# Attention with an int8 product behind it: two key tiles in one burst, and another order of scores and maxima

## The chip, the cores and the metric

The kernel runs on one core of one Trainium2 chip. The metric is the device time of one execution in microseconds, as the median of the runs. TensorE (PE in the profile, its weight loads PEld), VectorE (DVE), ScalarE (ACT), GpSimd (POOL) and SyncE (SP) each work through their own queue in order and wait for each other by semaphores.

## The reference

Eight batches of x, each 512 x 1024 (channels x positions), are projected with three weight matrices over the channels; attention with 16 heads of 32 channels and a mask over the keys follows; its result, seen as 512 rows of 1024, goes through a product with 1024 x 1024 int8 weights, each row quantised to int8 first, and x is added.

```python
Q, K, V = proj(Wq), proj(Wk), proj(Wv)          # "oc,bct->bto", then B,H,T,Dh
att = einsum("bhqd,bhkd->bhqk", Q, K) / sqrt(Dh) + b[0]
att = softmax(att * m + (1 - m) * -1e30, axis=-1)
y = einsum("bhqk,bhkd->bhqd", att, V)           # back to B, C, T
scale = max(abs(y).max(-1), 1e-7) / 127         # one row: one channel, 1024 positions
q = clip(round(y / scale), -128, 127)
out = x + float16((q @ weight.T) * scale * w_scale + bias)
```

## The kernel before

A first part (`project`) makes Q, K and V of all batches; it isn't touched. The second part (`attend`) has 32 steps, each one batch and a group of four heads. In a step there are 64 score units: two halves of 512 queries, eight key tiles of 128 keys, four heads. A unit is one matmul into one of three score banks (`scores`, L689), whose contraction runs over 100 rows: three parts of q and k, the mask's bias and two rows with the row maxima, so that the exponential (`exps`, ScalarE, L798) can be taken straight from the bank. A unit may use a bank again when the exponential three units before is done. A key tile of four exponentials is then multiplied with V by eight narrow matmuls of 32 columns that share the array (`weigh`, L716, a "burst"): a burst for tile k stands behind the last unit of tile k+1.

The row maxima for the step after are found beside that. For each of 32 pairs (head and 128 queries) two matmuls over 512 keys each (`row_max`, L127) fill one of two buffers of 1024 columns, called the ring, and VectorE reduces it to one column (`reduce_max`, L136). 64 maxima matmuls, or slots, thus stand beside the 64 units: unit, slot, unit, slot, with the bursts between. The ring's buffers are used in turn, and four more uses a step ("extras") take a turn too: the row sums of the halves (`sum_rows`, L726 and L729, behind slots SUMS_1 = 23 for the step before and SUMS_0 = 55), the turn of the int8 rows (`turn_q`, L740, behind 47) and the last product (`ffn`, L749, behind 51). A use waits until the use two before it has been read.

Half of the maxima (16 columns of 128 queries) are complete behind slots 19 and 51. With the row sums TensorE turns them (`turn_max`, L734); ScalarE takes a high part (`high_max`, L803), VectorE the rest (`low_max`, L878), and SP stores both as rows of `q_stack` (`store_max`, L609: two transfers of 16 runs of 512 B). Units 0 and 32 wait for the landing. ScalarE's queue also holds the copies of the weighted sums (`take_y`, L808), the rounding of the rows (`round_rows`, L814, behind units 37 and 39), their conversion (`make_ints`, L820, behind 41 and 43) and the issues of the loads for the next steps, of q behind units 24 to 26 and 38 to 40. VectorE's queue holds the reciprocals of the sums (`recip`, L885 and L888), their spreading (`spread`, L894, four slots behind the sums), the absolute maxima (L899) and the products' scaling (L922). GpSimd sums the exponentials of key tiles (L988), begins transfers that add a tile to another (L972, each waits for a burst) and normalises (L1007) and finishes the rows (L1013, L1016).

All orders are written out by hand: each engine has a function `step` that goes through t = 0 to 63.

Of the kernel before, what the change touches and what calls it, by code (L numbers as in the profile page):

```python
# [25 lines left out]
P = 128  # L26
# [36 lines left out]
SUMS_1, TURN_Q, FFN, SUMS_0 = 23, 47, 51, 55  # L63
# [3 lines left out]
SCORES = 3  # L67

# [7 lines left out]
def score_bank(t):  # L76

    return (t - (t > SUMS_1)) % SCORES


def score_before(t):

    if t == SUMS_1 + 1:
        return t - 1
    return t - 4 if SUMS_1 + 1 < t < SUMS_1 + 1 + SCORES else t - SCORES

# [417 lines left out]
def attend(nc, x, qk_d, v_d, bias_d, fw, ws_rep, fb_rep, out,  # L504
# [3 lines left out]
    with ExitStack() as ctx:  # L508
# [38 lines left out]
        maxT_done = sem("maxT_done")  # L547
# [8 lines left out]
        max_lo_done = sem("max_lo_done")  # L556
        recip_done = sem("recip_done")
# [15 lines left out]
        MAX_ROWS = 16 * 2  # L573
# [30 lines left out]
        def _(sp):  # L604
            def store_max(par, chunk):

                for part, rows in ((0, max_hi), (1, max_lo)):
                    dst = q_stack[par][ROW_MAX + part:ROW_MAX + part + 1, chunk, :, :]
                    sp.dma_start(dst.bitcast(F32), rows[:, chunk, :].bitcast(F32)).then_inc(max_rows[chunk], 16)  # L609
# [3 lines left out]
            def step(s, par, prev=True, main=True, ahead=True):  # L613
                if main:
                    sp.wait_ge(max_hi_done, 2 * s + 2)
                    sp.wait_ge(max_lo_done, 2 * s + 2)
                    store_max(par, 1)
                if ahead:
                    sp.wait_ge(max_hi_done, 2 * s + 3)
                    sp.wait_ge(max_lo_done, 2 * s + 3)  # L620
                    store_max(1 - par, 0)
# [21 lines left out]
        def _(pe):  # L643
            def taken(s, use):

                kind, t = use
                if not isinstance(s, int):
                    return True
                if kind == "max":
                    return 0 <= max_of_slot(s, t)[0] < STEPS  # L650
                return s < STEPS if t == SUMS_0 else 0 <= s <= STEPS if t == SUMS_1 else 0 <= s - 1 < STEPS

            def wait_ring(s, use):
# [5 lines left out]
                elif t in (SUMS_1, SUMS_0):  # L659
                    wait(pe, sums_out, 2 * s + (t == SUMS_0))  # L660
                    if not isinstance(s, int) or s + (t == SUMS_0) < STEPS:
                        pe.wait_ge(max_lo_done, 2 * s + (2 if t == SUMS_1 else 3))
# [5 lines left out]
            def take_ring(s, par, use):  # L668

                if isinstance(s, int) and (s < 0 or s == 0 and PLACE[use] < 2):  # L670
                    pe.wait_ge(neg_max_done, EARLY)
                    wait(pe, max_lo_done, s + 1)
# [78 lines left out]

            def step(s, par, prev=True, main=True, ahead=True):
                for t in range(UNITS):
                    if main:
                        scores(s, par, t)
                    if has_max(t, main, ahead):
                        next_max(s, par, t)
                    if t == GH - 1 and prev:
                        weigh(s - 1, 1 - par, QH * TT - 1)
                    if t % GH == GH - 1 and t > GH and main:  # L760
                        weigh(s, par, t // GH - 1)
                    use = ("extra", t)
                    if t == SUMS_1 and (prev or main):
                        buf = take_ring(s, par, use)
                        if main:
                            turn_max(s, 1, buf)
                        if prev:
                            sum_rows(s - 1, 1, buf)
                    if t == SUMS_0 and (main or ahead):
                        buf = take_ring(s, par, use)  # L770
                        if ahead:
                            turn_max(s + 1, 0, buf)
                        if main:
                            sum_rows(s, 0, buf)
                    if t == TURN_Q and prev:
                        turn_q(s - 1, take_ring(s, par, use))
                    if t == FFN and prev:
                        ffn(s - 1, take_ring(s, par, use))

            pe.wait_ge(const_set, 5)  # L780
# [3 lines left out]
        def _(act):  # L784
# [60 lines left out]
            def step(s, par, prev=True, main=True, ahead=True):  # L845
                for t in range(UNITS):
# [15 lines left out]
                    if t == SUMS_0 and ahead:  # L862
                        high_max(s + 1, 0, ring_of(par, ("extra", SUMS_0)))

            act.wait_ge(const_set, 5)
# [5 lines left out]
        def _(dve):  # L871
# [4 lines left out]
            def low_max(s, chunk, buf):  # L876
# [220 lines left out]
```

## Time and profile before

| | |
|---|---|
| median of 3 runs | 2441.62 us (2440.1 to 2443.0) |
| the profiled execution | 2440.84 us, of which the span is 2439.0 us |
| TensorE busy | 2387.2 us, 98% of the span |
| GpSimd, VectorE, ScalarE busy | 1672.1 us (69%), 1560.4 us (64%), 1346.3 us (55%) |
| granted clock of TensorE, mean | 0.993 |

The span is one execution as the profiler saw it, from its first to its last instruction. Busy time of TensorE is made of modelled ends of matmuls that overlap, so that distances between starts say more than lengths do. The steps of `attend` begin at 571.46 us.

### The profile page before, as it was taken

To read this page: it belongs to the slowest core of one execution; us is meant where nothing else is said; L and a number is where in the kernel's file an instruction comes from. 1 tells how busy PE (TensorE), PEld (TensorE's weight loads), DVE (VectorE), ACT (ScalarE), POOL (GpSimd) and SP (SyncE) were. 2 spreads that over 40 slices of the span, in tenths; PEclk is the share of its full clock that TensorE was granted. 3 is DMA by queue.
4 is the path that set the end of the run, shared out by engine and by line. 5 is a ranking of instruction groups with operands and counts; after the bars stand their busy time and mean duration, and the time that the engine had idled before them with its cause. 6 is when DMAs were issued, how large, how long until landed. Compare 5 with 4: busy or idle time off the path is not lost.

```text
span 2439.0 us, 37390 instructions
## 1 busy us (share of the span) xinstructions
PE 2387.2 (98%) x12376; PEld 1341.0 (55%) x12376; DVE 1560.4 (64%) x1683; ACT 1346.3 (55%) x2536; POOL 1672.1 (69%) x677
## 2 busy tenths in 40 slices
PE   8999999997999999999999999999999999999996
PEld 7888888884444444444444444444444444444442
DVE  3311111145777777777777777777777877777771
ACT  3222222214666666666666666666666666666664
POOL 3322223414778888888877888888788888887777
PEclk9999999998999999999999999999999999999999
DMA  6655555365677776777677777666776667776751
GB/s 243 252 200 199 214 193 195 147 211 126 147 160 160 157 157 147 157 159 159 151 159 159 156 160 156 157 151 150 160 160 155 155 150 160 160 155 154 157 111 44
DMA packets 143498, 396.55 MB, mean 163 GB/s; under 512 B 14584, under 2 KB 50424, under 8 KB 127296
## 3 DMA queue, kind: packets, MB, share of 16 engines
q0 software_dynamic: 18144, 132.13, 27.4%
q10 hardware_dynamic: 49312, 130.80, 22.8%
q1 hardware_dynamic: 75968, 132.74, 14.9%
q8 instruction: 34, 0.56, 0.1%
q14 instruction: 40, 0.33, 0.0%
HBM read 161.51 MB, written 100.93 MB: 108 GB/s over the span
## 4 chain that ended last, share of the span: by engine, by line
PE 67%; DMA 4%; issue 2%; POOL 2%; DVE 2%; ACT 0%; SPq 0%; ACTq 0%; POOLq 0%; DVEq 0%
PE score L689 21%; PE pv L716 18%; PE ring L127 18%; PE ring L749 4%; DMA q_stack<-max_lo 4%; PE ring L726 2%; PE ring L729 2%; DVE neg_max L136 1%; PE ring L740 1%; POOL acc L988 1%; PE ring L734 0%; DMA probs<-probs 0%; POOL acc L1000 0%; ACT probs L798 0%; SPq L609 0%
## 5 line engine op out<-in xcount | busy, mean ns | idle before, releaser
L798 ACT ACTIVATE probs<-score 128x512 f32<-128x512 f32 x2048 | 1074.7, 604 | 576.4 <-PE score L689 559.5
L136 DVE TENSOR_REDUCE neg_max<-ring 128x1 f32<-128x1024 f32 x1024 | 1208.4, 1220 | 230.8 <-PE ring L127 219.1
L689 PE MATMUL score<-q_stack,k_stack 100*128 100x512 f32 x2048 | 875.8, 429 | 23.9 <-DMA q_stack<-max_lo 16.6
L988 POOL TENSOR_TENSOR acc<-acc,probs 128x2048 f32<-128x2048 f32 x189 | 867.1, 4588 | 26.6 <-DMA probs<-probs 11.9
L127 PE MATMUL ring<-k_stack,q_stack 98*128 98x512 f32 x2048 | 810.6, 396 | 0.3 <-DVE neg_max L136 0.2
L689 PEld LDWEIGHTS score<-q_stack,k_stack 100*128 100x128 f32 x2048 | 387.3, 189 | 504.0 <-ACT probs L798 358.2
L716 PE MATMUL pv<-probs,v_in 128*32 128x512 f32 x4096 | 546.1, 605 | 0.0
L127 PEld LDWEIGHTS ring<-k_stack,q_stack 98*128 98x128 f32 x2048 | 390.8, 191 | 66.6 <-DVE neg_max L136 0.8
L988 POOL TENSOR_TENSOR acc<-probs 128x2048 f32<-128x2048 f32 x63 | 288.8, 4584 | 100.8 <-DMA probs<-probs 100.8
L479 POOL TENSOR_TENSOR q_stack<-x_raw,k_stack 128x1024 fp32r<-128x1024 f32 x28 | 67.7, 2450 | 294.7 <-ACT k_stack L364 294.7
L972 POOL DMA_DIRECT2D probs<-probs x126 | 108.2, 859 | 175.4 <-PE pv L716 168.2
L716 PEld LDWEIGHTS pv<-probs,v_in 128*32 128x32 f32 x4096 | 80.6, 108 | 184.7 <-ACT probs L798 162.6
L435 DVE TENSOR_TENSOR part_lo<-score,part_hi 128x512 fp32r<-128x512 f32 x24 | 16.4, 691 | 178.7 <-ACT part_hi L389 178.7
L491 POOL TENSOR_TENSOR part_lo<-k_scaled,part_hi 128x512 fp32r<-128x512 f32 x64 | 82.1, 1301 | 56.2 <-ACT part_hi L392 56.2
L749 PE MATMUL ring<-fw,qT 128*128 128x512 bf16 x512 | 117.8, 384 | 0.9 <-DVE qT L917 0.9
L1013 POOL TENSOR_TENSOR half<-prod,fb_rep 128x512 f16<-128x512 f32 x64 | 81.4, 1272 | 47.9 <-DVE prod L922 47.9
L291 PE MATMUL ring<-k_stack,w_hi 128*128 128x512 f32 x256 | 101.1, 395 | 0.0
L291 PE MATMUL ring<-k_stack,w_lo 128*128 128x512 f32 x256 | 101.1, 395 | 0.0
L291 PE MATMUL ring<-q_stack,w_hi 128*128 128x512 f32 x256 | 101.1, 395 | 0.0
L392 ACT ACTIVATE part_hi<-k_scaled 128x512 fp32r<-128x512 f32 x64 | 38.9, 628 | 111.3 <-DVE k_scaled L446 76.4
L885 DVE STREAM_TRANSPOSE sums_turned<-ring 128x512 f32<-128x512 f32 x64 | 45.9, 717 | 84.6 <-PE ring L729 84.6
L922 DVE SCALAR_TENSOR_TENSOR prod<-ring,scale,ws_rep 128x512 f32<-128x512 f32 x64 | 48.1, 751 | 80.8 <-PE ring L749 80.8
(95 smaller groups left out, 2026.6 us busy)
## 6 DMA issues: line engine op xcount, KB each, us to landing
probs<-probs POOLq DMA_DIRECT2D x126, 1024.0 KB, 8.0
k_stack<-qk_part ACTq DMA_DIRECT2D x93, 512.0 KB
q_stack<-qk_part ACTq DMA_DIRECT2D x183, 256.0 KB, 5.4
qk_part<-part_hi SPq DMA_DIRECT2D x64, 512.0 KB, 2.6
qk_part<-part_lo SPq DMA_DIRECT2D x64, 512.0 KB, 3.5
v_steps<-v_out SPq DMA_DIRECT2D x64, 256.0 KB, 2.2
res<-x ACTq DMA_DIRECT2D x32, 512.0 KB, 5.7
out<-res SPq DMA_DIRECT2D x64, 256.0 KB, 2.1
```

The source lines that it names most:

```text
L127: mm = pe.matmul(ring[:, half * N:(half + 1) * N], q_stack[par][0:ROW_MAX, chunk, h, qt * P:(qt + 1) * P], k_stack[par][0:ROW_MAX, h, half ...
L136: nc.vector.tensor_reduce(neg_max[:, pair // CHUNK, pair % CHUNK:pair % CHUNK + 1], ring[:, :], AX_X, ALU.max, negate=True).then_inc(neg_m ...
L291: return pe.matmul(bank[:, :], lhsT, rhs, start=(k == 0), stop=(k == 3 * CT - 1))
L479: nc.gpsimd.tensor_tensor(x_lo[par][:, a, :], x_raw[:, a, :], x_hi[par][:, a, :].bitcast(F32), ALU.subtract).then_inc(x_lo_done, 1)
L491: nc.gpsimd.tensor_tensor(part_lo[:, g % 2, th * N:(th + 1) * N], k_scaled[:, i % 2, :], part_hi[:, g % 2, th * N:(th + 1) * N].bitcast(F3 ...
L689: pe.matmul(score[score_bank(t)][:, :], k_stack[par][0:ROWS, h, kt * P:(kt + 1) * P], q_stack[par][0:ROWS, half, h, :], start=True, stop=T ...
L716: mm = pe.matmul(pv[h * DH:(h + 1) * DH, :], v_in[:, par, kt % TT, h * DH:(h + 1) * DH], probs[:, kt % RING, h, :], start=(kt % TT == 0), ...
L749: mm = pe.matmul(buf[:, cols], qT[:, tt, :], fw[:, tt, cols], start=(tt == 0), stop=(tt == TT - 1))
L798: nc.scalar.activation(probs[:, kt, h, :], score[score_bank(t)][:, :], ACT.Exp).then_inc(exp_done, 1)
L972: pool.dma_start(probs[:, b, :, :], probs[:, a, :, :], accum_op=ALU.add).then_inc(pair_done[i], 16)
L988: nc.gpsimd.tensor_tensor(acc[:, half, :, :], first, probs[:, tile, :, :], ALU.add).then_inc(acc_done, 1)
L1013: nc.gpsimd.tensor_tensor(half16[:, half, :], prod[:, half, :], fb_rep[:, cols], ALU.add).then_inc(half_done, 1)
```

## The change

TensorE's `step` no longer goes through units and slots in turn. It follows a fixed list, a cycle of eight scores (S) and eight maxima (M), `SSMMSSSMMSSMMSMM`, entered at its tenth place; eight cycles are a step. Behind every eighth maximum (slots 3, 11, 19, ..., 59) two key tiles are weighted in one burst, 16 narrow matmuls; by then three units more than the two tiles have been issued. The row sums move to slots 27 and 59, right behind a burst; the last product stays behind slot 51, which now is a burst's too, and the turn of q behind slot 47, in the middle of a cycle.

TensorE no longer turns the maxima. ScalarE makes the high parts straight from the column form (behind units 18 and 50), VectorE the low ones, both of 128 x 16, and VectorE turns both together in blocks of 32 x 32 (behind slots 21 and 51). SP stores them by four transfers, one for each 32 queries of a tile, whose runs are 128 B. VectorE's turn waits for the landing of the stores of the step before, SP for the turn. `ident` goes, which only TensorE's turn needed; the copies of the weighted sums move by one unit.

```diff
-SUMS_1, TURN_Q, FFN, SUMS_0 = 23, 47, 51, 55
+SUMS_1, TURN_Q, FFN, SUMS_0 = 27, 47, 51, 59
+CYCLE = "SSMMSSSMMSSMMSMM"
+ENTRY = 9
+ORDER = CYCLE[ENTRY:] + (UNITS // (2 * GH) - 1) * CYCLE + CYCLE[:ENTRY]
+BURST = GH - 1
+RESTART = SUMS_1
...
-    return (t - (t > SUMS_1)) % SCORES
+    return (t - (t >= RESTART)) % SCORES
...
-        max_hi = sb("max_hi", [CHUNK, 2, P], F32R)
-        max_lo = sb("max_lo", [CHUNK, 2, P], F32R)
-        ident = sb("ident", [P, P], F32)
+        max_parts = sb("max_parts", [P, 2, 2, CHUNK], F32R)
+        max_turned = sb("max_turned", [P, 2, 2 * CHUNK], F32)
...
             def store_max(par, chunk):
-                for part, rows in ((0, max_hi), (1, max_lo)):
-                    dst = q_stack[par][ROW_MAX + part:ROW_MAX + part + 1, chunk, :, :]
-                    sp.dma_start(dst.bitcast(F32), rows[:, chunk, :].bitcast(F32)).then_inc(max_rows[chunk], 16)
+                rows = q_stack[par][ROW_MAX:ROW_MAX + 2, chunk, :, :].rearrange("r h (a g j) -> r h a g j", g=P // DH, j=DH)
+                for g in range(P // DH):
+                    sp.dma_start(rows[:, :, :, g, :].bitcast(F32), max_turned[g * DH:(g + 1) * DH, chunk, :]).then_inc(max_rows[chunk], 16)
...
                 if main:
-                    sp.wait_ge(max_hi_done, 2 * s + 2)
-                    sp.wait_ge(max_lo_done, 2 * s + 2)
+                    sp.wait_ge(max_turn_done, 2 * s + 2)
                     store_max(par, 1)
...
-            def turn_max(s, chunk, buf):
-                pe.wait_ge(neg_max_done, PAIRS * s + CHUNK * (chunk + 1))
-                pe.transpose(buf[0:CHUNK, N:N + P], neg_max[:, chunk, :], ident[:, :]).then_inc(maxT_done, 1)
...
+            def after_burst(s, par, t, prev, main):
+                use = ("extra", t)
+                if t == SUMS_1 and prev:
+                    sum_rows(s - 1, 1, take_ring(s, par, use))
+                if t == SUMS_0 and main:
+                    sum_rows(s, 0, take_ring(s, par, use))
+                if t == FFN and prev:
+                    ffn(s - 1, take_ring(s, par, use))
...
             def step(s, par, prev=True, main=True, ahead=True):
-                for t in range(UNITS):
-                    if main:
-                        scores(s, par, t)
-                    if has_max(t, main, ahead):
-                        next_max(s, par, t)
...
+                unit = slot = 0
+                for kind in ORDER:
+                    if kind == "S":
                         if main:
+                            scores(s, par, unit)
+                        unit += 1
+                        continue
+                    if has_max(slot, main, ahead):
+                        next_max(s, par, slot)
+                    if slot == TURN_Q and prev:
+                        turn_q(s - 1, take_ring(s, par, ("extra", TURN_Q)))
+                    if slot % (2 * GH) == BURST:
+                        if slot == BURST and prev:
+                            for kt in (QH * TT - 2, QH * TT - 1):
+                                weigh(s - 1, 1 - par, kt)
+                        if slot > BURST and main:
+                            for kt in (slot // GH - 2, slot // GH - 1):
+                                weigh(s, par, kt)
+                        after_burst(s, par, slot, prev, main)
+                    slot += 1
...
-            def high_max(s, chunk, buf):
-                act.wait_ge(maxT_done, 2 * s + chunk + 1)
-                wait(act, max_rows[chunk], MAX_ROWS * s)
-                nc.scalar.activation(max_hi[:, chunk, :], buf[0:CHUNK, N:N + P], ACT.Copy).then_inc(max_hi_done, 1)
+            def high_max(s, chunk):
+                act.wait_ge(neg_max_done, PAIRS * s + CHUNK * (chunk + 1))
+                wait(act, max_turn_done, 2 * (s - 1) + chunk + 1)
+                nc.scalar.activation(max_parts[:, chunk, 0, :], neg_max[:, chunk, :], ACT.Copy).then_inc(max_hi_done, 1)
...
-                    if t == 3 and prev:
+                    if t == 2 and prev:
                         take_y(s - 1, 1)
-                    if t == SUMS_1 and main:
-                        high_max(s, 1, ring_of(par, ("extra", SUMS_1)))
-                    if t == 35 and main:
+                    if t == 18 and main:
+                        high_max(s, 1)
+                    if t == 34 and main:
                         take_y(s, 0)
...
+                    if t == 50 and ahead:
+                        high_max(s + 1, 0)
...
+            def turn_max(s, chunk):
+                dve.wait_ge(max_lo_done, 2 * s + chunk + 1)
+                wait(dve, max_rows[chunk], MAX_ROWS * s)
+                nc.vector.transpose(max_turned[:, chunk, :],
+                                    max_parts[:, chunk, :, :].rearrange("p a b -> p (a b)").bitcast(F32)).then_inc(max_turn_done, 1)
...
-                    if t == SUMS_1 and main:
-                        low_max(s, 1, ring_of(par, ("extra", SUMS_1)))
+                    if t == 21 and main:
+                        low_max(s, 1)
+                        turn_max(s, 1)
+                    if t == FFN and ahead:
+                        low_max(s + 1, 0)
+                        turn_max(s + 1, 0)
...
```

## Rows read from the trace of the kernel before

**Rows 1.** The page: busy time and share of the span, each engine.
```profile
PE 2387.2 (98%) x12376; PEld 1341.0 (55%) x12376; DVE 1560.4 (64%) x1683; ACT 1346.3 (55%) x2536; POOL 1672.1 (69%) x677
```

**Rows 2.** Timeline: start us, length us, engine, line. First and 32nd step's first score.
```profile
571.46 0.79 PE L689 MATMUL score<-q_stack,k_stack 100*128 100x512 f32 x1 [9.71 <-DMA q_stack<-max_lo]
...
2356.46 0.50 PE L689 MATMUL score<-q_stack,k_stack 100*128 100x512 f32 x1
```

**Rows 3.** Timeline of TensorE, one key tile inside a step.
```profile
1503.88 1.07 PE L716 MATMUL pv<-probs,v_in 128*32 128x512 f32 x8
1504.87 0.50 PE L689 MATMUL score<-q_stack,k_stack 100*128 100x512 f32 x1
1505.21 0.40 PE L127 MATMUL ring<-k_stack,q_stack 98*128 98x512 f32 x1
...
1506.61 0.39 PE L127 MATMUL ring<-k_stack,q_stack 98*128 98x512 f32 x1
1506.93 1.07 PE L716 MATMUL pv<-probs,v_in 128*32 128x512 f32 x8
```

**Rows 4.** Timeline of TensorE, row sums behind a burst.
```profile
1510.98 0.28 PE L734 MATMUL ring<-ident,neg_max 128*16 128x128 f32 x1
1511.18 1.07 PE L726 MATMUL ring<-probs,ones 128*32 128x512 f32 x8
1512.07 1.04 PE L729 MATMUL ring<-acc,ones 128*32 128x512 f32 x8
1513.04 0.50 PE L689 MATMUL score<-q_stack,k_stack 100*128 100x512 f32 x1
```

**Rows 5.** Timeline of TensorE, the turn of q and the last product.
```profile
1531.16 1.06 PE L716 MATMUL pv<-probs,v_in 128*32 128x512 f32 x8
...
1532.59 0.48 PE L689 MATMUL score<-q_stack,k_stack 100*128 100x512 f32 x1
...
1534.63 1.07 PE L716 MATMUL pv<-probs,v_in 128*32 128x512 f32 x8
...
1538.91 0.59 PE L689 MATMUL score<-q_stack,k_stack 100*128 100x512 f32 x1
```

**Rows 6.** Timeline of ScalarE: exponentials, and a rounding between them.
```profile
1505.49 2.06 ACT L798 ACTIVATE probs<-score 128x512 f32<-128x512 f32 x4 [0.99 <-PE score L689]
...
1525.02 1.06 ACT L798 ACTIVATE probs<-score 128x512 f32<-128x512 f32 x2
1525.97 0.81 ACT L814 ACTIVATE y<-y,magic,inv_scale 128x512 f32<-128x512 f32 x1
...
1526.68 1.08 ACT L798 ACTIVATE probs<-score 128x512 f32<-128x512 f32 x2
```

**Rows 7.** Timeline of TensorE in the last step, without maxima.
```profile
2379.17 0.97 PE L689 MATMUL score<-q_stack,k_stack 100*128 100x512 f32 x3
2380.44 0.50 PE L689 MATMUL score<-q_stack,k_stack 100*128 100x512 f32 x1 [0.30 <-ACT probs L798]
```

**Rows 8.** Timeline: maxima matmuls and VectorE's reductions of them.
```profile
1502.62 0.40 PE L127 MATMUL ring<-k_stack,q_stack 98*128 98x512 f32 x1
...
1503.05 2.36 DVE L136 TENSOR_REDUCE neg_max<-ring 128x1 f32<-128x1024 f32 x2 [0.70 <-PE ring L127]
...
612.22 2.36 DVE L136 TENSOR_REDUCE neg_max<-ring 128x1 f32<-128x1024 f32 x2 [0.70 <-PE ring L127]
...
614.62 0.19 PEld L127 LDWEIGHTS ring<-k_stack,q_stack 98*128 98x128 f32 x1 [0.41 <-DVE neg_max L136]
```

**Rows 9.** Timeline: issue of a store of the maxima on SP's queue.
```profile
1512.52 1.36 SPq L609 DMA_DIRECT2D q_stack<-max_lo  x1
```

**Rows 10.** One tile's view, the stores of the low parts.
```profile
DMA to landing us min/median/max: 1.8/4.2/8.2
```

**Rows 11.** Groups: count, busy us, mean ns of one, idle us before.
```profile
L136 DVE TENSOR_REDUCE neg_max<-ring 128x1 f32<-128x1024 f32 x986 | 1162.6, 1220 | 216.4 <-PE ring L127 204.8
...
L888 DVE RECIPROCAL recips<-sums_turned 128x16 f32<-128x16 f32 x62 | 15.7, 253 | 2.1
```

More of the change, by code:

```diff
@@ L76, in score_bank @@
 def score_bank(t):
-    return (t - (t > SUMS_1)) % SCORES
+    return (t - (t >= RESTART)) % SCORES
 def score_before(t):
-    if t == SUMS_1 + 1:
+    if t == RESTART:
         return t - 1
-    return t - 4 if SUMS_1 + 1 < t < SUMS_1 + 1 + SCORES else t - SCORES
+    return t - 4 if RESTART < t < RESTART + SCORES else t - SCORES
 def max_of_slot(s, t):
@@ L546, in attend @@
         pv_done = sem("pv_done")
-        maxT_done = sem("maxT_done")
         sum_done = sem("sum_done")
@@ L556, in attend @@
         max_lo_done = sem("max_lo_done")
+        max_turn_done = sem("max_turn_done")
         recip_done = sem("recip_done")
@@ L571, in attend @@
         res_done = sem("res_done")
-        MAX_ROWS = 16 * 2
+        MAX_ROWS = 16 * P // DH
         def halves_before(s, half):
@@ L650, in taken @@
                     return 0 <= max_of_slot(s, t)[0] < STEPS
-                return s < STEPS if t == SUMS_0 else 0 <= s <= STEPS if t == SUMS_1 else 0 <= s - 1 < STEPS
+                return 0 <= s < STEPS if t == SUMS_0 else 0 <= s - 1 < STEPS
             def wait_ring(s, use):
@@ L659, in wait_ring @@
                 elif t in (SUMS_1, SUMS_0):
-                    wait(pe, sums_out, 2 * s + (t == SUMS_0))
-                    if not isinstance(s, int) or s + (t == SUMS_0) < STEPS:
-                        pe.wait_ge(max_lo_done, 2 * s + (2 if t == SUMS_1 else 3))
+                    pe.wait_ge(sums_out, 2 * s + (t == SUMS_0))
                 elif t == TURN_Q:
@@ L671, in take_ring @@
                     pe.wait_ge(neg_max_done, EARLY)
-                    wait(pe, max_lo_done, s + 1)
                 else:
@@ L750, in ffn @@
                     mm.then_inc(ffn_done, 1)
-            def step(s, par, prev=True, main=True, ahead=True):
-                for t in range(UNITS):
-                    if main:
-                        scores(s, par, t)
-                    if has_max(t, main, ahead):
-                        next_max(s, par, t)
[L758 to L764, printed above, removed]
-                        if main:
[L766 to L778, printed above, removed]
@@ L781, in _ @@
+            pe.wait_ge(const_set, 4)
             all_steps(pe, step)
@@ L861, in step @@
                         make_ints(s - 1, (t - 41) // 2)
-                    if t == SUMS_0 and ahead:
-                        high_max(s + 1, 0, ring_of(par, ("extra", SUMS_0)))
-            act.wait_ge(const_set, 5)
+                    if t == 50 and ahead:
+                        high_max(s + 1, 0)
+            act.wait_ge(const_set, 4)
             act.wait_ge(stack_set, 4)
@@ L874, in _, with low_max @@
             nc.vector.memset(magic[:, 1:2], -MAGIC).then_inc(const_set, 1)
-            def low_max(s, chunk, buf):
+            def low_max(s, chunk):
                 dve.wait_ge(max_hi_done, 2 * s + chunk + 1)
-                nc.vector.tensor_tensor(max_lo[:, chunk, :], buf[0:CHUNK, N:N + P],
-                                        max_hi[:, chunk, :].bitcast(F32), ALU.subtract).then_inc(max_lo_done, 1)
+                dve.wait_ge(neg_max_done, PAIRS * s + CHUNK * (chunk + 1))
+                nc.vector.tensor_tensor(max_parts[:, chunk, 1, :], neg_max[:, chunk, :],
+                                        max_parts[:, chunk, 0, :].bitcast(F32), ALU.subtract).then_inc(max_lo_done, 1)
+            def turn_max(s, chunk):
[3 more added lines that the diff above has]
+                                    max_parts[:, chunk, :, :].rearrange("p a b -> p (a b)").bitcast(F32)).then_inc(max_turn_done, 1)
             def recip(s, half, buf):
@@ L946, in step @@
                             scale_product(s - 1, half, ring_of(par, ("extra", FFN)))
-                    if t == SUMS_0 and ahead:
-                        low_max(s + 1, 0, ring_of(par, ("extra", SUMS_0)))
                     if t == SUMS_0 and main:
@@ L957, in _ @@
         def _(pool):
-            for eye in (ident, ident16):
-                nc.gpsimd.memset(eye[:, :], 0.0).then_inc(zeroed, 1)
-            for k, eye in enumerate((ident, ident16)):
-                pool.wait_ge(zeroed, 2)
-                nc.gpsimd.affine_select(out=eye[:, :], in_=eye[:, :], compare_op=ALU.not_equal, fill=1.0, base=0,
-                                        pattern=[[-1, P]], channel_multiplier=1).then_inc(const_set, 1)
+            nc.gpsimd.memset(ident16[:, :], 0.0).then_inc(zeroed, 1)
+            pool.wait_ge(zeroed, 1)
+            nc.gpsimd.affine_select(out=ident16[:, :], in_=ident16[:, :], compare_op=ALU.not_equal, fill=1.0, base=0,
+                                    pattern=[[-1, P]], channel_multiplier=1).then_inc(const_set, 1)
             set_rows(nc, q_stack[1], k_stack[1], stack_set)
```

4 lines of the change are left out of this document (1 added, 3 removed).

## The prediction

> **What bounds the kernel now.** I read the page first: TensorE is busy for 98% of the span, every other engine for far less [rows 1]. So a gain has to come out of TensorE's own time, and a loss can come from anything that makes it wait. From the timeline I took the first score of the first and of the last of the 32 steps [rows 2]: 2356.46 - 571.46 = 1785.0 us for 31 steps, 57.58 us each. All of the change lies in these steps.
>
> The timeline of TensorE inside a step [rows 3] shows a period of one key tile: four scores and four maxima alternate, each 0.235 us behind the one before (from 1505.21 to 1506.61 are six places), then eight weighting matmuls (one "burst"). The period is 1506.93 - 1503.88 = 3.05 us. The first score starts 0.99 us behind the burst's start and the maximum after it 0.34 us later (0.10 more than normal, because the weights can't be loaded ahead); the burst starts 0.32 us behind the last maximum. Eight plain places would be 1.88 us, so a burst costs 1.17.
>
> Where the row sums follow [rows 4], the second of two blocks of narrow matmuls in a row starts 0.89 us behind the first, and nothing is paid for a change of shape between them. The transposition of the maxima costs 0.20 and stands between two narrow blocks; from it to the next score are 2.06 us. The turn of q adds 1.43 - 0.99 = 0.44 to a period, the last product 4.28 - 0.99 = 3.29 [rows 5]. Together a step without waits is 16 x 3.05 + 2 x 2.06 + 0.44 + 3.29 = 56.65 us; the other 0.9 of 57.58 are waits that are there already.
>
> **What the change removes.** (a) Eight of sixteen bursts lose their own entry and exit: two tiles in one burst take 0.89 + 0.99 = 1.88 us to the next score, so a pair of tiles without waits takes 6.10 - 1.17 + 0.89 = 5.82 us. That is 0.28 x 8 = 2.25 us a step. (b) The transposition goes, and the sums stand right behind a burst: 2 x 0.89 = 1.78 instead of 2.06 for each of two, 0.56 us a step. Together 2.8 us a step, 87 us in 31 steps, if nothing waits.
>
> On the cost of changing the shape, the page on array packing of the Trainium skill (TensorEngine Tiling (Array Packing), Performance Considerations, "PSUM Bottleneck") warns of the other side: what TensorE gains is lost where PSUM can't be emptied as fast. By the busy shares of [rows 1] neither emptying engine would be full and the sum would be the 87 us gained; by the places in the cycle, which the next part works out, the rule holds.
>
> **What it adds: waits inside the cycle.** The new cycle is SS MM SSS MM SS MM S MM burst, with still three score banks and two maxima buffers. Durations first. ScalarE's exponential starts 0.62 us behind a first score [rows 3, 6], 1504.87 and 1505.49; queued, it takes 0.475 us from start to start (1525.02, two, then 1525.97), and one lasts 0.60. A score three places later may start 0.05 after its end. VectorE's reduction starts 0.43 us behind the second maximum matmul of a pair, lasts 1.22, and 1.14 lie between two starts (2.36 for two) [rows 8, 11]. A maximum that has to wait for its buffer starts its weight load 0.04 to 0.05 us behind the reduction's end (612.22 + 2.36 = 614.58, then 614.62). Whoever waits pays 0.10 on top for the load that wasn't ahead, as the first score does.
>
> One cycle, from its first score:
> - S0 0, S1 0.34, M 0.57 and 0.81, S2 1.04. S3 is due at 1.28 and needs the first exponential, 0.62 + 0.60 + 0.05 = 1.27: it starts in time but without its weights loaded, 0.10 lost. The last step, which has no maxima, shows this wait itself: the fourth score starts 1.27 us after the first and TensorE idles 0.30 [rows 7].
> - S4 is due at 1.61 and needs the second exponential: 1.095 + 0.60 + 0.05 = 1.75. Lost 0.14 + 0.10.
> - M 2.09 and 2.32 (second pair), S5 2.56, S6 2.79, M 3.02 and 3.26, S7 3.49: no wait, the exponentials needed are over by then (the fifth at 3.12).
> - The fourth pair is due at 3.73 and takes the second pair's buffer. That reduction starts 2.32 + 0.43 = 2.75 and ends 3.97: start 4.02, lost 0.29 + 0.10.
> - The burst starts at 4.36 + 0.32 = 4.68, the next cycle at 6.56.
>
> So waits take 0.74 us of each cycle: 6.56 against 6.10 before, 8 x 0.74 = 5.9 us a step. In the old alternating order this didn't occur, since a score came only every 0.47 us and the two pairs of a tile had the burst behind them.
>
> **Work that falls into the cycles.** The roundings behind units 37 and 39 hold ScalarE 0.71 us each (1525.97 to 1526.68) [rows 6], the two conversions behind 41 and 43 I take at nearly the same. With three banks each delays a score: the rounding makes S41 wait about 0.73, which hides that cycle's 0.39 of the fourth pair (net 0.35). The conversion behind 43 makes S47 wait 0.6 more, and the turn of q takes a maxima buffer in the middle of the cycle (0.2 more): 1.15 together. The y copies (behind units 2 and 34) and the high halves of the maxima (18 and 50) come where ScalarE has nothing to do until the burst ends; free. If a reduction is late there, what queues behind is the next cycle's first exponential, which has about 0.6 us of room. On VectorE the low halves and the turn, of 16 and 32 columns, are not in the trace in this form; they cost more than nothing and less than a reduction over 1024 columns (1.22), and nearest is the row of 16 columns, 253 ns [rows 11]. Two of these, 0.45 us, stand ahead of the second pair's reduction in one cycle, which the fourth pair waits for: 0.1 us more, since that reduction had 0.29 to wait for its matmuls anyway. Total 1.25 us, in place of the 0.9 of before.
>
> **The stores of the maxima.** SP now issues four small stores instead of two, behind one wait. For the second half of the queries an issue took up to 1.36 us and the landing a median of 4.2 us, 8.2 at most [rows 9, 10]. The turned values are ready some 2.9 us into the cycle of units 19 to 26 (the first reduction ends at 2.46, and 0.45); the score that needs them, unit 32, is S5 of the next cycle and due 6.56 + 1.78 + 2.6 - 2.9 = 8.0 us later. Four issues of 0.5 (cheapest) and 4.2 make 6.2: no wait. Two at 0.52 and two at 1.36 make 3.8 and, with 4.2 to 8.2, 8.0 to 12: between nothing and 4 us late. ScalarE's three loads of q are issued in the same microseconds, so I don't take nothing; part of such a wait is absorbed by the 0.39 of the pair behind it. I take 0.4 us a step, bounds 0 and 3.6.
>
> The page on DMA (DMA: Bandwidth & Descriptors, Specifications) asks for 512 B per transfer and says that smaller ones cost a read-modify-write; the runs here shrink from 512 to 128 B. The same page confines the slowness to HBM ("Why small descriptors are slow (HBM only)"), and no row here separates the two. By the first the upper bound would be nearer.
>
> POOL waits four units longer for the factor (made behind unit 31 instead of 27): it is busy 69% over the span [rows 1] and its sums now have until slots 27 and 59; nothing taken. Start and end: four issues instead of two, one constant less, under 2 us.
>
> **Sum.** 56.65 - 2.8 + 5.9 + 1.25 + 0.4 = 61.4 us a step, 3.8 more than 57.58; times 31 is +118 us. The profiled execution took 2440.84 us (span 2439.0), 0.8 under the median of 2441.62. I predict 2560 us.
>
> **Rivals.**
> 1. The waits are smaller. If the 0.10 of the weight load were not paid (0.30 of the 0.74 in a cycle), 8 x 0.30 = 2.4 us a step go, about 2485 to 2510 with the stores on time. Against it: the load is seen uncovered behind each burst.
> 2. Faster: if the exponentials or reductions let go of their banks some 0.3 us before the recorded ends, or TensorE ran past the waits, what is left is 2.8 - 0.35: 2365 us. It decides from waits under 0.30 us a cycle. Against it: both releases are seen at the recorded end [rows 7, 8].
> 3. The stores of the second half come 2 us or more late each step: 2560 + 31 x 1.6 = 2610 or more. The long issue speaks for it [rows 9], the median landing against it [rows 10].
> 4. The double burst saves nothing, each eight keeping its 1.17: 2560 + 70 = 2630. The sums speak against it [rows 4].
>
> **Chances.** Forecast 0.62 (2530 to 2590); rival 1 0.14; rival 3 0.11; rival 4 0.02; rival 2 0.08; something that cancels to within 0.2% (about what a measurement of this kernel can tell from no change) 0.03. So faster 0.08, same 0.03, slower 0.89. The range leaves out the faster cases, the cheapest of rival 1 and the dearest of 3: 2500 to 2620.
>
> **What would show it.** In the changed profile: eight bursts of 16 a step, 1.88 us to the next score; a cycle of 6.5 us with TensorE's weight loads waiting for ScalarE at the fourth and fifth score and for VectorE at the fourth pair; steps of 61 to 62 us; fewer than 95% busy. Cycles of 5.8 us would prove me wrong; so would a wait for stores that exceeds those in the cycles.

## The result, and the profile after

The changed kernel takes 2717.87 us against 2442.31 (medians of four runs each): ratio 1.113, 95% interval 1.111 to 1.115. Slower was forecast, but 2560 us; the loss is 276 us where 118 were worked out.

The page of the changed kernel: busy time and share of the span, then the chain that ended last (the work followed back from the last instruction), as shares by engine and by line.
```profile
span 2713.1 us, 37400 instructions
PE 2490.2 (92%) x12312; PEld 1362.4 (50%) x12312; DVE 1574.7 (58%) x1747; ACT 1331.5 (49%) x2536; POOL 1669.5 (62%) x675
...
PE 47%; DMA 9%; DVE 8%; issue 5%; ACT 5%; SPq 3%; POOL 3%; POOLq 0%; ACTq 0%; DVEq 0%
PE pv L715 16%; PE ring L132 13%; PE score L688 12%; DMA q_stack<-max_turned 9%; DVE neg_max L141 7%; PE ring L744 4%; SPq L613 3%; ACT probs L798 3%; POOL acc L996 2%; PE ring L728 1%; PE ring L725 1%; ACT q_int L820 1%; ACT y_raw L808 1%; DMA probs<-probs 1%; ACT y L814 1%
```
The same chain of the kernel before, by engine:
```profile
PE 67%; DMA 4%; issue 2%; POOL 2%; DVE 2%; ACT 0%; SPq 0%; ACTq 0%; POOLq 0%; DVEq 0%
```
TensorE was busy 98% before [rows 1] and had 67% of the chain; now it is busy 92% and has 47%, and 9% of the chain are the stores of the turned maxima, 8% VectorE, 5% ScalarE.

The timeline of TensorE, the first score of the first and of the 32nd step:
```profile
572.33 0.76 PE L688 MATMUL score<-q_stack,k_stack 100*128 100x512 f32 x1 [15.72 <-DMA q_stack<-max_turned]
...
2629.66 0.67 PE L688 MATMUL score<-q_stack,k_stack 100*128 100x512 f32 x2
```
(2629.66 - 572.33) / 31 = 66.37 us a step, against 57.58 [rows 2] and 61.4 forecast. 31 x 8.79 = 272 us, of the 274 us between the two profiled spans, lie in these steps.

A plain cycle, the eight scores of units 11 to 18 (TensorE's timeline, matmuls of one line in a row merged):
```profile
1575.47 0.73 PE L688 MATMUL score<-q_stack,k_stack 100*128 100x512 f32 x2
1576.04 0.63 PE L132 MATMUL ring<-k_stack,q_stack 98*128 98x512 f32 x2
1576.51 1.13 PE L688 MATMUL score<-q_stack,k_stack 100*128 100x512 f32 x3
1577.48 0.63 PE L132 MATMUL ring<-k_stack,q_stack 98*128 98x512 f32 x2
1577.95 0.67 PE L688 MATMUL score<-q_stack,k_stack 100*128 100x512 f32 x2
1578.46 0.63 PE L132 MATMUL ring<-k_stack,q_stack 98*128 98x512 f32 x2
1578.93 0.40 PE L688 MATMUL score<-q_stack,k_stack 100*128 100x512 f32 x1
1579.43 0.74 PE L132 MATMUL ring<-k_stack,q_stack 98*128 98x512 f32 x2
1580.10 1.92 PE L715 MATMUL pv<-probs,v_in 128*32 128x512 f32 x16
1581.95 0.73 PE L688 MATMUL score<-q_stack,k_stack 100*128 100x512 f32 x2
```
It lasts 6.48 us; 6.56 were worked out. The double burst reaches the next score after 1.85 us (1.88 worked out; two single bursts take 0.99 each and are entered twice [rows 3]). The weight loads of the same cycle show what it waits for (in brackets: idle of the load unit, and who ended it):
```profile
1576.65 0.19 PEld L688 LDWEIGHTS score<-q_stack,k_stack 100*128 100x128 f32 x1 [0.19 <-ACT probs L798]
1577.14 0.19 PEld L688 LDWEIGHTS score<-q_stack,k_stack 100*128 100x128 f32 x1 [0.30 <-ACT probs L798]
...
1579.43 0.30 PEld L132 LDWEIGHTS ring<-k_stack,q_stack 98*128 98x128 f32 x2 [0.54 <-DVE neg_max L141]
```
The fourth and the fifth score wait for ScalarE, the fourth pair of maxima for VectorE, as forecast. What wasn't forecast in this size stands at unit 32 of the same step:
```profile
1592.28 0.63 PE L132 MATMUL ring<-k_stack,q_stack 98*128 98x512 f32 x2
1596.08 0.73 PE L688 MATMUL score<-q_stack,k_stack 100*128 100x512 f32 x2 [3.17 <-DMA q_stack<-max_turned]
1596.64 0.63 PE L132 MATMUL ring<-k_stack,q_stack 98*128 98x512 f32 x2
1597.11 0.57 PE L688 MATMUL score<-q_stack,k_stack 100*128 100x512 f32 x1
1597.47 1.05 PE L132 MATMUL ring<-k_stack,q_stack 98*128 98x512 f32 x2
1598.46 2.95 PE L715 MATMUL pv<-probs,v_in 128*32 128x512 f32 x16
1601.34 0.73 PE L688 MATMUL score<-q_stack,k_stack 100*128 100x512 f32 x2
```
Unit 32 was due at 1592.75 and starts at 1596.08, released by the stores. After that the same work is slower: the burst takes 2.88 us to the next score instead of 1.85. The view by windows shows the clock of these stretches (length, busy us of TensorE, its loads, VectorE, ScalarE, GpSimd, then the granted clock, the transfers' share and GB/s):
```profile
1592.00:1596.00 4.00, 0.91 (x3) 0.43 (x3) 2.57 (x3) 1.35 (x3) 1.14 (x1) 1.00 1.02 218
1596.00:1599.00 3.00, 2.92 (x11) 1.67 (x15) 1.66 (x2) 1.62 (x3) 3.00 (x2) 0.69 0.03 12
1599.00:1602.00 3.00, 3.00 (x19) 0.97 (x12) 1.76 (x4) 0.51 (x2) 2.92 (x2) 0.74 0.00 0
1602.00:1605.00 3.00, 2.51 (x10) 1.36 (x9) 2.11 (x2) 3.00 (x7) 3.00 (x1) 1.00 0.23 63
```
TensorE stood still for 3.3 us, and the clock was granted at 0.69 and 0.74 in the next two stretches of 3 us, a mixture of its two levels, before it was 1.00 again. From unit 32 to the next cycle are 5.26 us here (1601.34 - 1596.08) and 4.00 in the plain cycle (1581.95 - 1577.95), so the stall costs about 1.3 us more than its own length. This step is a mild one: in the mean of steps 2 to 31 unit 32 starts 4.1 us later than in e1 below, where it waits for no store, and what follows it takes 2.0 us longer, together some 6 us a step. Over the span the granted clock is 0.963 (0.993 before).

The stores' side of it, the queues of SP and ScalarE and GpSimd's transfer in that step (start, time of the issues, how many):
```profile
1584.87 4.48 SPq L613 DMA_DIRECT2D q_stack<-max_turned  x4
...
1584.98 1.62 ACTq L107 DMA_DIRECT2D q_stack<-qk_part  x2
...
1586.66 1.23 ACTq L107 DMA_DIRECT2D q_stack<-qk_part  x1
...
1582.63 0.88 POOL L980 DMA_DIRECT2D probs<-probs  x1 [3.40 <-PE pv L715]
```
And what the transfer engines did with it, from the packets of the same traces, 16th step (times in us; the added transfer is GpSimd's 1 MB between key tiles):

```
kernel                  added transfer ends  packets of the stores       loads of q run
before                  1460.7               1459.0 to 1460.7 (32x512B)  from 1460.2
after                   1591.0               1590.2 to 1594.8 (128x128B) 1589.3 to 1594.3
e9_before_four_stores   1511.4               1510.9 to 1513.5 (64x256B)  from 1511.0
e2_q_loads_later        1502.9               1502.5 to 1503.5 (128x128B) from 1507.6
```
In each of these kernels the stores don't start until the added transfer is near its end, whenever they are issued (at most 2.7 us ahead of it in steps 2 to 31). Before, both were in their queue by then; they began 1.2 us ahead of the loads of q and were through in 1.7 us. Now the loads are issued while the four stores still are (4.48 us for four) and begin 0.9 us ahead of them, and the same 16 KB take 4.6 us between them.

### The profile page after: what moved, and what is told of

It is laid out like the page before. It is cut to its first block, busy times and chain, and to the rows that moved or that the text cites. A ratio compares the mean times of both kernels' runs of the same rounds, so it can differ in the third digit from the quotient of the medians.

```text
span 2713.1 us, 37400 instructions
## 1 busy us (share of the span) xinstructions
PE 2490.2 (92%) x12312; PEld 1362.4 (50%) x12312; DVE 1574.7 (58%) x1747; ACT 1331.5 (49%) x2536; POOL 1669.5 (62%) x675
## 4 chain that ended last, share of the span: by engine, by line
PE 47%; DMA 9%; DVE 8%; issue 5%; ACT 5%; SPq 3%; POOL 3%; POOLq 0%; ACTq 0%; DVEq 0%
PE pv L715 16%; PE ring L132 13%; PE score L688 12%; DMA q_stack<-max_turned 9%; DVE neg_max L141 7%; PE ring L744 4%; SPq L613 3%; ACT probs L798 3%; POOL acc L996 2%; PE ring L728 1%; PE ring L725 1%; ACT q_int L820 1%; ACT y_raw L808 1%; DMA probs<-probs 1%; ACT y L814 1%
## 5 line engine op out<-in xcount | busy, mean ns | idle before, releaser
L688 PE MATMUL score<-q_stack,k_stack 100*128 100x512 f32 x2048 | 790.9, 446 | 169.4 <-DMA q_stack<-max_turned 133.8
L132 PE MATMUL ring<-k_stack,q_stack 98*128 98x512 f32 x2048 | 690.9, 417 | 31.1 <-DVE neg_max L141 17.5
L688 PEld LDWEIGHTS score<-q_stack,k_stack 100*128 100x128 f32 x2048 | 368.9, 191 | 605.9 <-issue 302.0
L715 PE MATMUL pv<-probs,v_in 128*32 128x512 f32 x4096 | 529.5, 637 | 0.0
L715 PEld LDWEIGHTS pv<-probs,v_in 128*32 128x32 f32 x4096 | 111.5, 114 | 275.3 <-issue 206.1
L1015 POOL TENSOR_TENSOR y<-y_raw,factor 128x512 f32<-128x512 f32 x64 | 81.8, 1278 | 139.8 <-DVE factor L902 139.8
L808 ACT ACTIVATE y_raw<-pv 128x512 f32<-128x512 f32 x64 | 38.4, 600 | 172.2 <-PE pv L715 164.9
```

What stands on the lines that cost most here:

```text
L132: mm = pe.matmul(ring[:, half * N:(half + 1) * N], q_stack[par][0:ROW_MAX, chunk, h, qt * P:(qt + 1) * P], k_stack[par][0:ROW_MAX, h, half ...
L688: pe.matmul(score[score_bank(t)][:, :], k_stack[par][0:ROWS, h, kt * P:(kt + 1) * P], q_stack[par][0:ROWS, half, h, :], start=True, stop=T ...
L715: mm = pe.matmul(pv[h * DH:(h + 1) * DH, :], v_in[:, par, kt % TT, h * DH:(h + 1) * DH], probs[:, kt % RING, h, :], start=(kt % TT == 0), ...
L1015: nc.gpsimd.tensor_tensor(y[:, half * N:(half + 1) * N], y_raw[:, half, :], factor[:, half, :], ALU.mult).then_inc(y_done, 1)
```

## The experiments

**Is it the late rows?** `e1_no_late_rows` lets the second half's scores read 98 rows, without those of the maxima:

```diff
-                if t % (UNITS // 2) == 0:
+                if t == 0:
                     pe.wait_ge(max_rows[half], MAX_ROWS * (s + 1))
+                rows = ROWS if half == 0 else ROW_MAX
...
```


> The changed kernel, but the scores of the second half of the queries contract over 98 rows instead of 100: the two rows with the row maxima are left out there, so unit 32 and those behind it wait for no store (the stores are still made). Theory A (the stores of the second half come some 3.3 us late in each step and the stall lets TensorE's clock fall, together about 5 us a step): steps of 61.3 us instead of 66.4, about 2560 us, clock back to about 0.99. Rival B (the waits inside the cycles and VectorE's work cost more than was worked out, the stores little): 2650 us or more.

Measured: 2532.53 us (ratio to before 1.038, 1.035 to 1.040), 60.47 us a step, clock 0.993. The late rows, with what the clock lost by them, cost 5.9 us a step, 185 us. Theory A holds, and the price is higher than it said: the time lies 28 us under the 2560 set. Of the loss 90 us remain.

**What makes them late?** `e2_q_loads_later` moves three issues on ScalarE's queue:

```diff
-                if ahead and t in (24, 25, 26):
+                if ahead and t in (33, 34, 35):
...
```


> The changed kernel, but ScalarE issues the three loads of q of the second half behind units 33 to 35 instead of 24 to 26. Theory A1 (the stores, once they run, share the transfer engines with these 768 KB and so take 4.6 us instead of 1): unit 32 waits under 0.5 us, 2570 to 2590 us. Rival A2 (only the 1 MB that GpSimd's transfer adds between key tiles holds the stores back): 2700 us or more.

Measured: 2533.06 us (1.038, 1.036 to 1.040), 60.48 us a step: the same as e1, with all of the kernel's work done, and 37 us under the range that theory A1 set. From the waits of this kernel over the span (us in total, times, longest):
```profile
PEld score L688 <- ACT probs L798: 252.4, 772, 1.0
...
PEld ring L132 <- DVE neg_max L141: 130.1, 220, 4.2
...
PE score L688 <- DMA q_stack<-max_turned: 16.1, 2, 15.7
```
Of the stores only the wait at the start is left (15.7 us, one of two); the other two are the cycles' own. The 128 packets take 1.0 us when no loads run beside them (the table above), so their small size alone is not what costs. The page DMA: Bandwidth & Descriptors of the Trainium skill (Queues, rings and completion order) says that a transfer engine goes round its queues and drains a whole packet, typically of 9 to 17 descriptors, before it switches. The trace agrees as far as it goes: in the changed kernel stores and loads of q start among each other from 1590.2 to 1594.1, 4.6 us for the stores against 1.0 alone; and from the first store's issue at 1584.87 to 1589.3 nothing of either moved beside the added transfer, whose 1 MB the profile records as pieces of 8 KB, eight for each of 16 engines if they are spread evenly. Whether such eight are one packet in the page's sense no run shows.

`e3_pair_transfer_later` leaves the loads and holds that added transfer back:

```diff
+                if (half, i) == (0, 1):
+                    pool.wait_ge(max_rows[1], MAX_ROWS * (s + 1))
```


> The changed kernel, but GpSimd begins the second of the two 1 MB transfers of the first half only when the stores of the maxima have landed. Theory A2 (that transfer holds the stores back): stores land within 5 us of the turn, no wait at unit 32, about 2560 us, if GpSimd's sums can begin some 6 us later without being late. Rival A1 (the loads of q hold them back): unit 32 still waits 2 us or more, 2640 us or more.

Measured: 2621.14 us (1.074, 1.070 to 1.078), between the two forecasts. For unit 32 theory A2 holds. Distances between the starts of two scores, from the traces (us, means of steps 2 to 31; the last column is the whole step, first to 32nd, as above):

| | plain cycle, units 11 to 19 | units 27 to 35 | units 35 to 43, with the roundings | step |
|---|---|---|---|---|
| changed kernel | 6.48 | 12.59 | 6.90 | 66.37 |
| e1, no late rows | 6.48 | 6.48 | 6.88 | 60.47 |
| e2, loads of q later | 6.48 | 6.48 | 6.88 | 60.48 |
| e3, added transfer later | 6.47 | 6.51 | 9.01 | 63.47 |

The cycle of unit 32 is as short in e3 as without any wait. What e3 loses lies elsewhere: 2.1 us in the cycle with the roundings, and 0.7 in front of unit 0, which now waits for its own stores. The waits of e3 in three steps (960 to 1150 us) show the first:
```profile
POOL probs L982 <- DMA q_stack<-max_turned: 36.3, 3, 12.6
...
PE score L688 <- ACT probs L798: 6.7, 7, 1.8
DVE absmax L907 <- POOL y L1017: 5.4, 3, 2.4
...
ACT y L814 <- DVE inv_scale L920: 2.7, 3, 1.3
```
GpSimd stands 12 us a step in front of the held transfer, its finished rows come late to VectorE's absolute maxima, and ScalarE's rounding and the scores behind it wait. So either of the two neighbours out of the way relieves the stores of unit 32.

**The turn alone.** `e4_turn_alone` is the changed kernel with the old order, sums and bursts put back, so that VectorE's turn and its four stores are what is left:

```diff
-SUMS_1, TURN_Q, FFN, SUMS_0 = 27, 47, 51, 59
+SUMS_1, TURN_Q, FFN, SUMS_0 = 23, 47, 51, 55
...
-                for kind in ORDER:
+                for t in range(UNITS):
+                    if main:
+                        scores(s, par, t)
+                    if has_max(t, main, ahead):
+                        next_max(s, par, t)
...
-                    if t == 18 and main:
+                    if t == 21 and main:
                         high_max(s, 1)
```

> The kernel before with the row maxima turned by VectorE and stored by four transfers alone: scores and maxima alternate, one tile a burst, sums behind 23 and 55, high parts behind units 21 and 51. Theory A (four stores in 128 B runs land 11 to 12 us behind the turn, and unit 32 comes 10 to 11 us behind it in this order): 0.5 to 2 us late a step, less the 0.5 us that the transposition and its change of shape cost, 2440 to 2500 us. Rival (the late landing belongs to the new order alone): 2425 to 2435 us.

Measured: 2588.64 us (1.061, 1.059 to 1.063), 62.31 us a step. The direction is A's, the size far over its 2500 us: half of the change's loss comes with the turn even where the order stays. From the view of the turned tile in this kernel, who waited for it:
```profile
  PE score L688: 125.8, 32
  PEld score L688: 21.4, 5
```
`e6_turn_alone_q_later` is the same with the loads of q behind units 33 to 35, and `e5_before_q_later` the kernel before with nothing but that.

> The row maxima turned by VectorE in the old order (e4_turn_alone), with the loads of q behind units 33 to 35. Theory A1 (late stores, because they share the transfer engines with these loads, are all that the turn costs): no wait at unit 32, and with TensorE's transposition gone 1 us a step less than the kernel before, 2405 to 2425 us. Rival (VectorE's and ScalarE's small operations cost as well): above 2445 us.

> The kernel before with nothing changed but the place of ScalarE's three loads of q of the second half, behind units 33 to 35 instead of 24 to 26. Theory: in the old kernel too the loads hold ScalarE (issues of 0.9 to 1.35 us) and unit 32 waits 0.17 us for its rows; 0.3 to 0.7 us a step go, 2418 to 2432 us. Rival: these waits are hidden elsewhere, 2438 to 2443 us.

Measured: e6 2411.06 us (0.988, 0.986 to 0.990), e5 2424.55 us (0.994, 0.992 to 0.995). Both as expected. The turn on VectorE is worth 13 us once its stores run free (e5 less e6), and 148 us of loss when they don't (e4 less the kernel before); and the old kernel carried a wait of the same kind. e6 beats both kernels.

**How many stores?** `e9_before_four_stores` keeps TensorE's turn and splits each of its two stores in two:

```diff
-                    dst = q_stack[par][ROW_MAX + part:ROW_MAX + part + 1, chunk, :, :]
-                    sp.dma_start(dst.bitcast(F32), rows[:, chunk, :].bitcast(F32)).then_inc(max_rows[chunk], 16)
+                    dst = q_stack[par][ROW_MAX + part:ROW_MAX + part + 1, chunk, :, :].rearrange("r h (a j) -> r h a j", j=P)
+                    for g in range(2):
+                        cols = slice(g * P // 2, (g + 1) * P // 2)
+                        sp.dma_start(dst[:, :, :, cols].bitcast(F32), rows[:, chunk, cols].bitcast(F32)).then_inc(max_rows[chunk], 16)
```


> The kernel before, TensorE's turn and all, with each of its two stores of the maxima split into two of 64 columns (runs of 256 B): four issues on SP's queue instead of two, in the same bytes and at the same place; the loads of q stay behind units 24 to 26. Theory C (it is the number of issues: the third and fourth fall behind the loads of q in the transfer queues): unit 32 waits 1 to 3 us a step and the clock falls, 2475 to 2560 us. Rival D (it is the runs of 128 B or the place where VectorE makes the rows): 2440 to 2450 us.

Measured: 2545.54 us (1.042, 1.040 to 1.044), in theory C's range. TensorE's timeline at unit 32 in this kernel:
```profile
1511.58 1.07 PE L718 MATMUL pv<-probs,v_in 128*32 128x512 f32 x8
1514.89 0.49 PE L691 MATMUL score<-q_stack,k_stack 100*128 100x512 f32 x1 [2.25 <-DMA q_stack<-max_lo]
```
The same bytes in two issues more, and unit 32 comes 3.31 us behind its burst instead of the 0.99 of a plain one [rows 3]. Neither 128 B nor VectorE's turn is needed for a late landing, so rival D is out as the whole cause. But with the issues the packets double too (32 to 64 for the second half), and this run doesn't tell the two apart. From the first to the last packet the second half's stores take 1.4 us in the kernel before, 3.6 in e9 and 4.9 in the changed kernel, all with the loads of q beside them (medians of steps 2 to 31).

One more thing changes with the turn, and no run takes it by itself. For each store of the kernel before and of e9 the traces record 16 updates of its semaphore (1024 for 64 stores), for each store of the changed kernel three (384 for 128); and of the changed kernel's packets of 128 B at most four are under way at once, of the old kernel's of 512 B up to eleven. That reads as if a new store, whose target is two rows, lay on few of the 16 transfer engines and an old one on all. So why the new stores suffer so much from the loads of q stays open between issues, packets and this spread.

**The waits in the cycle.** What is left in e2 is the order: 2533.06 against 2411.06 for the old order with the same turn and loads, 3.9 us a step. `e7_even_order` changes only the cycle in e2 (the first pair of lines); `e8_half_reductions` only VectorE's reduction in e2, which leaves out half of the keys (the second):

```diff
-CYCLE = "SSMMSSSMMSSMMSMM"
+CYCLE = "SSMMSSMMSSMMSSMM"
...
-    nc.vector.tensor_reduce(neg_max[:, pair // CHUNK, pair % CHUNK:pair % CHUNK + 1], ring[:, :],
+    nc.vector.tensor_reduce(neg_max[:, pair // CHUNK, pair % CHUNK:pair % CHUNK + 1], ring[:, 0:N],
```


> e2_q_loads_later with the cycle SSMMSSMMSSMMSSMM instead of SSMMSSSMMSSMMSMM. Theory B (what is left of the loss are the waits in the cycle): the fourth and fifth score then have two maxima ahead of them and wait for no exponential, and seven places instead of six lie between the second pair and the fourth, so that 0.15 us of 0.37 of its wait are left; a cycle of about 6.1 instead of 6.47 us, 2.8 us a step, about 2445 us. Rival (the loss comes from elsewhere, POOL, ScalarE's extras or the burst itself): within 20 us of 2533.

> e2_q_loads_later with VectorE reducing only the first 512 of a pair's 1024 columns (the maxima then leave out half of the keys; all matmuls stay), so that a reduction lasts 0.7 instead of 1.22 us. Theory B: the fourth pair of a cycle no longer waits for its buffer, 0.37 us a cycle and some 0.2 at the turn of q go, 3.1 us a step, about 2437 us; the waits of the scores for the exponentials stay. Rival: the time of the cycle is set by the scores alone and what the maxima give back the scores take, above 2510 us.

Measured: e7 2459.12 us (1.008, 1.006 to 1.009), 58.06 us a step; e8 2463.37 us (1.009, 1.008 to 1.011), 58.10. Each takes away the greater part of the 93 us by which e2 is over the kernel before (2440.2 us beside it), as theory B says, 74 and 70 us; the two overlap and can't be added. Both fall short of what I had set, by 14 and 26 us. In e8 some of that are stores again: its scores wait 34 us for them over the span, 17 in e2.

To see what the double burst itself is worth, most of the waits can be taken away at once: `e10_even_half_reductions` is e7 with the halved reductions of e8, and `e11_no_waits_left` also has the second half's scores read 98 rows, with the edit of e1.

> e7_even_order with VectorE reducing only 512 of 1024 columns (the maxima leave out half of the keys). Theory B: the waits of maxima for their buffers go, the waits of scores at about 0.1 us each stay, 56.2 us a step and about 2400 us, hardly better than the old order without any of it (2411 us). Rival (the double burst pays once nothing waits for VectorE): 2370 us or less.

> e10_even_half_reductions with the scores of the second half contracting over 98 rows, the two rows with the maxima left out there (so both the reductions are halved and no store is waited for at unit 32). Theory B: what made e10 slower than forecast is only unit 32, which now comes sooner behind the turn and waits 2 to 2.7 us for its rows; without that 56.3 us a step, about 2400 us, still within 15 us of the old order with the same turn (2411 us). Rival (something else in e10, GpSimd's sums or the clock): 2440 us or more.

Measured: e10 2486.68 us (1.018, 1.016 to 1.021), slower than e7 and a miss. TensorE's timeline of e10 shows why:
```profile
1473.27 0.63 PE L132 MATMUL ring<-k_stack,q_stack 98*128 98x512 f32 x2
1473.74 0.40 PE L688 MATMUL score<-q_stack,k_stack 100*128 100x512 f32 x1
1475.86 0.49 PE L688 MATMUL score<-q_stack,k_stack 100*128 100x512 f32 x1 [1.72 <-DMA q_stack<-max_turned]
```
The faster cycles bring unit 32 nearer to the turn, and the stores, which come when the added transfer ends, are late again. e11 without that is 2377.73 us (0.975, 0.973 to 0.976), 55.45 us a step: 22 us under what I had set, and 33 us under e6. So the double burst does give TensorE time, and the waits for score banks and maxima buffers took it back. (The old order with halved reductions wasn't run. But two plain key tiles take 2 x 3.05 = 6.10 us there [rows 3], all of them places and bursts without a wait, so that a shorter reduction has nothing to give them; the plain cycle of e11 takes 5.89 us, mean of steps 2 to 31.)

## Why the prediction was wrong

- **What bounds the kernel, and the gain of the double burst:** right. 1.85 us to the next score against 1.88 worked out; where most waits are gone, in e11, the cycle is 5.89 us against 5.82 worked out without any.
- **Waits inside the cycle:** right in place and size. 6.48 us against 6.56 (the first exponential starts 0.53 us behind its score in the cycle shown, 1576.00, where 0.62 was taken), and the three waits stand where the recurrence put them. Without the stores' wait the step was to be 61.4 - 0.4 = 61.0 us; e1 and e2 have 60.5.
- **Roundings and conversions:** right, though no run changed them alone. In e2 (means of steps 2 to 31) the cycle with the roundings is 0.40 us longer than the plain one (0.35 worked out), the cycle with the conversion, the turn of q and the last product 4.59; less 0.44 and 3.29 for the last two [rows 5] that leaves 0.86 (0.8 worked out).
- **The step that failed is the price of the stores**, "I take 0.4 us a step, bounds 0 and 3.6". It measured 5.9 us, 5.5 more, which over 31 steps is 170 us and more than the whole miss of 158. The time that the stores had was worked out rightly: unit 32 comes 7.9 us behind the first issue in e2, where it doesn't wait (8.0 worked out). What they take was mis-sized: 12.2 us in the changed kernel (medians of steps 2 to 31), the upper end of "8.0 to 12". Two things went wrong. First, I took a median landing of 4.2 us over 64 stores [rows 10], and these are two kinds: in the trace of before the second half's low parts land 6.9 us behind their issue (median, 5.2 to 8.2), the first half's 1.8. Nor is 1.36 us [rows 9] the longest issue; the view that [rows 10] comes from has one of 2.07:
```profile
L609 SPq DMA_DIRECT2D q_stack<-max_lo x64: 577/1329/2069, 569.6 to 2376.0; - x64
```
The upper end, four slow issues and the slow landing, was in the rows; I chose near the lower. Second, no term stood for the clock: of the 6 us a step 4.1 are the wait itself, and 2.0 come behind it, where the 4 us from unit 32 to the next cycle become 6 at a lower granted clock. Part of the wait was to be absorbed by the 0.39 of the pair behind it; of that nothing is left to see.
- **The signs set beforehand:** the bursts, the cycle, its waits and the busy share (92%) came as written, the step (66.4 against 61 to 62) didn't. Of the two signs of being wrong, a wait for stores that exceeds those in the cycles was all but there: 4.1 us a step against 8 x 0.66 (6.48 - 5.82), and 6 with what follows it.
- **The rivals:** rival 3 named the mechanism, with 2610 us "or more" and a chance of 0.11; it was what happened, beside the forecast's own. Rival 1 (smaller waits) is out by the cycle of 6.48 us, rival 4 (no saving in the double burst) by the 1.85 us and e11, rival 2 (faster) by the result.
- **The rule of the Trainium skill on small transfers** (DMA: Bandwidth & Descriptors, Specifications), by which the upper bound was nearer: the bound was nearer, but that this was the cause isn't shown, since 128 runs of 128 B take 1.0 us alone. The same page of the Trainium skill keeps the slowness to HBM ("Why small descriptors are slow (HBM only)"), and the packets alone agree with that; beside the loads of q, where they take 4.6 us, no run separates their size from their number.
- **"POOL ... nothing taken"**: no run contradicts it for the change as it stands; e3, where GpSimd's wait in front of the held transfer lasts 12 us a step, goes past the room that it has.

## What to carry to other kernels

Where a queue's landing decides a start, read the landings of just that transfer, and look at what is issued beside it and ahead of it: two more small issues in the old kernel, with twice the packets, cost 103 us, and moving three loads by nine units took 185 us off the new one. An engine's share of busy time doesn't show what a burst meets: with three score banks and two buffers, the order of producers has to be laid against the consumers' start-to-start times, place by place, and this recurrence was right to 0.1 us a cycle. A stall of TensorE should be priced with what its clock does afterwards.

## What the runs showed of the hardware

- In the 16th step of the changed kernel the 1 MB transfer that adds on its way, which ended at 1591.0, ran without a packet of the two other queues from the first store's issue at 1584.87 to 1589.3; the stores began at 1590.2. In the 17th step of e10, where that transfer ended at 1533.8, store packets came in pairs from 1530.2 on, and 103 of 128 began behind its end.
- After 3.3 us of standing still TensorE's granted clock was 0.69 and 0.74 in two stretches of 3 us, and a burst of 16 took 2.88 instead of 1.85 us.
- An issue of a store on SP's queue has a median of 1.16 us in the changed kernel (0.61 to 1.56, 256 issues) and of 0.62 in e3, where the added transfer waits for the stores.
- 128 packets of 128 B from four stores took 1.0 us alone (e2) and 4.6 us with 768 KB of loads on another queue.
- A store of the changed kernel, from 32 rows into two, had three recorded updates of its semaphore; one of the kernel before, from 16 rows into one, 16.
